# A transformer decoder in one program: biases added in PSUM and a new order in the first attention, and logits with standing weights

## The reference

```python
def _L0_attn_ref(x, ...):                      # 16 heads of 16
    q_in = linear(x, Wq_w, Wq_b).transpose(0, 2, 1)
    Q3 = conv1d(q_in, convq_w, convq_b, (1, 1))
    Q = linear(concat([q_in, Q3]), qproj_w, qproj_b)        # K likewise
    V = linear(x, Wv_w, Wv_b)
    tau = sigmoid(conv1d(gelu(conv1d(x_conv, tau1_w, tau1_b, groups=D)), tau2_w, tau2_b))
    # delta likewise
    scores = einsum('bhqd,bhkd->bhqk', Q, K) / sqrt(DK) * tau[..., None] + delta[:, :, None, :]
    out = einsum('bhqk,bhkd->bhqd', softmax(scores), V)
    return linear(out, out_w, out_b)
...
def _L0_ffn_ref(x, W_router, b_router, ...):
    logits = x_flat @ W_router.T + b_router                 # 4096 tokens, 8 experts, top 2
...
def _L1_ffn_ref(x, gate_query, log_temp, ...):
    gate_logits = einsum('bnd,ed->ben', x, gate_query)      # 16 experts
    affinity = _sinkhorn(gate_logits / exp(log_temp))
```

## Time and profile before

| | us |
|---|---|
| median of 3 runs | 2656.15 (2645.31 to 2673.6) |
| profiled execution | 2657.47 |
| its span | 2655.8 |
| granted TensorE clock, share of full speed, over the span | 0.912 |

### The profile page before, as it was taken

How to read it: one execution, slowest core, us unless ns; L and a number is a source line. 1 busy time by engine, 2 the same in 40 slices (tenths; PEclk the granted TensorE clock), 3 DMA queues, 4 the chain that set the end, 5 groups by cost and what they waited for, 6 DMA issues and landing times. The chain is left out here.

```text
span 2655.8 us, 46285 instructions
## 1 busy us (share of the span) xinstructions
PE 2191.8 (83%) x16966; PEld 1564.2 (59%) x16966; DVE 1637.7 (62%) x3322; ACT 1190.9 (45%) x1892; POOL 1057.1 (40%) x1203
## 2 busy tenths in 40 slices
PE   7588888887677729993899997995299999999996
PEld 6355555554455617872566666885167676767674
DVE  4578777785788665651777764555655555555552
ACT  1344445553211216651555553323264647474742
POOL 3976677660000012313555411210244545454533
PEclk9799999998887759996999997996599999999998
DMA  4000000000000113321001100003143434343422
GB/s 205 1 1 1 0 0 0 0 0 1 9 6 5 64 66 121 124 92 42 25 24 27 21 1 15 15 10 126 57 109 97 99 97 99 97 99 97 99 66 32
DMA packets 62560, 135.92 MB, mean 51 GB/s; under 512 B 10688, under 2 KB 46736, under 8 KB 55568
## 3 DMA queue, kind: packets, MB, share of 16 engines
q0 software_dynamic: 30976, 52.45, 9.7%
q1 hardware_dynamic: 31504, 82.41, 8.9%
HBM read 100.22 MB, written 34.60 MB: 51 GB/s over the span
## 5 line engine op out<-in xcount | busy, mean ns | idle before, releaser
L2957 ACT ACTIVATE f_h<-bank,f_b 128x512 f32<-128x512 f32 x256 | 175.9, 687 | 280.5 <-PE bank L176 273.3
L176 PE MATMUL ring<-f_w2hi,f_hidhi 128*128 128x256 f16 x1024 | 280.0, 273 | 6.0 <-DVE f_hidlo L2994 3.7
L2994 DVE TENSOR_TENSOR f_hidlo<-f_h,f_hidhi 128x512 f16<-128x512 f32 x256 | 177.3, 692 | 173.2 <-ACT f_hidhi L2958 172.0
L176 PE MATMUL ring<-f_w2hi,f_hidlo 128*128 128x256 f16 x1024 | 279.9, 273 | 0.0
L176 PE MATMUL ring<-f_w2lo,f_hidhi 128*128 128x256 f16 x1024 | 279.8, 273 | 0.0
L3048 POOL DMA_INDIRECT out<-f_y,f_to_row x128 | 211.8, 1655 | 47.7 <-issue 34.1
L176 PE MATMUL bank<-f_xthi,f_w1hi 128*128 128x512 f16 x512 | 195.2, 381 | 4.9 <-DVE f_w1lo L2977 4.9
L176 PE MATMUL bank<-f_xtlo,f_w1hi 128*128 128x512 f16 x512 | 195.1, 381 | 0.0
L176 PE MATMUL bank<-f_xthi,f_w1lo 128*128 128x512 f16 x512 | 195.1, 381 | 0.0
L1755 POOL COPY c_from_row<-c_token 128x5 uint32 (+1 forms) x8 | 1.5, 184 | 435.0 <-POOLq L1482 356.3
L2958 ACT ACTIVATE f_hidhi<-bank,f_b 128x512 f16<-128x512 f32 x256 | 173.9, 679 | 0.0
(11 more groups left out here) (519 smaller groups left out, 6001.7 us busy)
## 6 DMA issues: line engine op xcount, KB each, us to landing
f_raw<-in_e_w SPq DMA_DIRECT2D x32, 1024.0 KB
c_raw<-in_e_w SPq DMA_DIRECT2D x16, 1024.0 KB, 6.0
slots_out<-c_y POOLq DMA_DIRECT2D x8, 640.0 KB, 3.7
x<-in_x SPq DMA_DIRECT2D x1, 4096.0 KB, 23.9
tokens<-c_xn SPq DMA_DIRECT2D x16, 256.0 KB, 2.3
out<-x SPq DMA_DIRECT2D x1, 4096.0 KB, 13.7
tokens<-f_xn SPq DMA_DIRECT2D x16, 256.0 KB, 2.2
wb<-in_wb SPq DMA_DIRECT2D x1, 3096.0 KB, 31.8
```

The costliest lines, as they stand in the source:

```text
L176: mm = pe.matmul(out, left[a], right[b], start=first and n == 0, stop=last and n == 2)
L2957: act.activation(h32[n % 4][:, :], src, ACT.Gelu_apprx_tanh, bias=bias).then_inc(sig["h_full"], 1)
L2994: dve.tensor_tensor(hid_v[1][:, it, at], h32[n % 4][:, :], hid_v[0][:, it, at], ALU.subtract).then_inc(sig["h_lo"], 1)
```

## The change

In `attention_weights` DVE also splits the two rows of biases (v and output) into three bf16 parts that add up to them, and puts part k into partition k of `bias_parts`; POOL fills `ones`. In the attention a product of `ones` with `bias_parts`, accumulated into the same PSUM bank, adds the bias. The normalisation, v's copy and one of the four copies of weighed values go from DVE to ACT, and all three orders change. The logits of both stages come from one class, `EntryLogits`: the weights, padded to 32 columns, are loaded, and x moves in 256 columns, four entries side by side in four column tiles; the result, experts by tokens, is turned back. It has sixteen xn, written out without loops, and the stores are waited for one block later (`choose_experts`, `choose_tokens`). The store of x comes after those of xn.

```diff
@@ attention_weights, DVE @@
+                order.step(dve.tensor_copy(thirds[0][:, :], both))
+                order.wait()
+                order.step(dve.tensor_tensor(left[:, :], both, thirds[0][:, :], ALU.subtract))
+                order.wait()
+                order.step(dve.tensor_copy(thirds[1][:, :], left[:, :]))
+                order.wait()
+                dve.tensor_tensor(thirds[2][:, :], left[:, :], thirds[1][:, :], ALU.subtract)
+                order.step(dve.tensor_scalar(parts, thirds[0][:, :], here[:, 0:1], None, ALU.mult))
+                for k in (1, 2):
+                    order.wait()
+                    order.step(dve.scalar_tensor_tensor(out=parts, in0=thirds[k][:, :], scalar=here[:, k:k + 1],
+                                                        in1=parts, op0=ALU.mult, op1=ALU.add))
@@ first_attention, PE @@
+                def bias(out, n):
+                    return pe.matmul(out, mem.ones[:, :], mem.bias_parts[:, n * D:(n + 1) * D], start=False, stop=True)
...
                 def half(u, i, w, j, w_before, v):
                     rows(u, i, 0, w_before)
+                    if w_before:
+                        turn_weighed(other(u), w_before)
                     if v:
                         turn_x(u, v, w_before)
                     rows(u, i, 1, w_before)
-                    if w_before:
-                        turn_weighed(other(u), w_before)
                     rows(u, i, 2, w_before)
+                    if w:
+                        project_qk(w, j, 0)
                     if w_before:
                         turn_o(other(u), w_before, v)
-                    if w:
-                        project_qk(w, j, 0)
                     rows(u, i, 3, w_before)
                     if w:
                         project_qk(w, j, 1)
...
+                    rows(u, i, 6, w_before)
+                    if w:
+                        tau_delta(w, j, v)
+                    rows(u, i, 7, w_before)
+                    if w:
+                        project_qk(w, j, 4)
+                        sum_tau_delta(w, j)
+                        project_qk(w, j, 5)
+                    turn_again(u, i)
+                    if w:
+                        project_qk(w, j, 6)
+                        project_qk(w, j, 7)
+                    columns_of_scores(u, i, w, j, w_before, 0)
                     if w_before:
                         output(other(u), w_before)
+                    for c in (1, 2, 3):
                         columns_of_scores(u, i, w, j, w_before, c)
+                    weigh(u, i, 0)
+                    if w:
+                        turn_queries(w, j, 1)
+                    columns_of_scores(u, i, w, j, w_before, 4)
+                    if w:
+                        project_v(w, j)
+                    columns_of_scores(u, i, w, j, w_before, 5)
+                    weigh(u, i, 1)
+                    columns_of_scores(u, i, w, j, w_before, 6)
+                    if w:
+                        turn_queries(w, j, 0)
+                    columns_of_scores(u, i, w, j, w_before, 7)
+                    weigh(u, i, 2)
+                    if w:
+                        for t in (1, 0):
+                            turn_keys(w, j, t)
                     weigh(u, i, 3)
@@ first_attention, ACT: norm, copy_v and copy_weighed are new @@
                     if v:
+                        norm(u, v)
                         pad_x(u, v)
-                    if w:
-                        gelu(w, j)
                     if w_before:
                         copy_o(other(u), w_before)
                     if w:
+                        gelu(w, j)
...
+                    exponentials(u, i, 0)
+                    if w:
+                        high_queries(w, j)
+                    for c in range(1, 5):
                         exponentials(u, i, c)
                     if w:
-                        high_queries(w, j)
-                    for c in range(4, HP):
+                        copy_v(w, j)
+                    for c in range(5, HP):
                         exponentials(u, i, c)
                     if w:
                         copy_turned_keys(w, j)
+                    copy_weighed(u, i, 2)
@@ first_attention, DVE, the new lines of half (removed ones left out) @@
                     maximum(u, i, 0)
                     if w_before:
                         divide(other(u), w_before)
+                    for s in range(1, 8):
+                        maximum(u, i, s)
+                    stack_maxima(u, i)
+                    if w:
+                        take_td(w, j)
+                        take_q(w, j)
+                    copy_again(u, i)
+                    if w:
+                        scale_queries(w, j)
+                        take_k(w, j)
+                        stack_queries(w, j)
+                    if w_before:
+                        update(other(u), w_before)
+                    if w:
+                        stack_keys(w, j)
+                    take_weighed(u, i, 0)
+                    if w:
+                        copy_queries(w, j, 1)
                     if v:
                         low_x(u, v)
                     take_weighed(u, i, 1)
                     if w:
+                        copy_queries(w, j, 0)
                         copy_keys(w, j)
                     take_weighed(u, i, 3)
@@ EntryLogits @@
+            for h in range(KT):
+                for p in range(self.R):
+                    mm = pe.matmul(bank[4 + g % 2][32 * p:32 * p + 32, 0:S], self.w[:, h * 32:(h + 1) * 32],
+                                   tiles(self.xn_t[g % 2][p][:, :], KT)[:, h, :], start=h == 0, stop=h == KT - 1,
+                                   tile_position=(0, 32 * p), skip_group_check=True)
...
+        for g in range(G + 2):          # PE
+            if g < G:
+                turn(g)
+            if 1 <= g <= G:
+                multiply(g - 1)
+            if g >= 2:
+                turn_back(g - 2)
...
+        norm(0)                         # DVE
+        for g in range(1, G):
+            norm(g)
+            copy_by_expert(g - 1)
+            if g >= 2:
+                take(g - 2)
+        copy_by_expert(G - 1)
+        for g in (G - 2, G - 1):
+            take(g)
```

More of the change, by code:

```diff
@@ L263, in attention_weights @@
         cb = ctx.enter_context(nc.sbuf_tensor("fold_cb", [P, 2 * KT * P], F32))
+        thirds = [ctx.enter_context(nc.sbuf_tensor(f"fold_third{k}", [P, 2 * D], BF16)) for k in range(3)]
+        left = ctx.enter_context(nc.sbuf_tensor("fold_left", [P, 2 * D], F32))
         banks = mem.banks
@@ L782, in half @@
                         project_qk(w, j, 1)
-                    if w_before:
-                        output(other(u), w_before)
                     rows(u, i, 4, w_before)
@@ L1387, in router_logits @@
+def router_logits(nc, mem, dram, xn, logits, stored):
+    with ExitStack() as ctx:
+        work = EntryLogits(nc, mem, dram, "c", xn, ctx, tiles(mem.w("router"), KT), E0, stored)
+        by_entry = logits[:, :].rearrange("q (b t e) -> q b t e", t=NT, e=E0)
         with nc.Block() as block:
@@ L1405, in _ @@
             @block.scalar
             def _(act):
[L1407 to L1412 removed]
+                work.scalar(act)
             @block.sync
             def _(sp):
[L1416 to L1420 removed]
@@ L1432, in pair @@
-                def pair(i, now, last):
-                    if not last:
-                        norm(now)
-                    for p in range(R):
-                        dve.wait_ge(sig[f"logits_made{p}"], now)
-                        for t in range(NT):
-                            ins = dve.tensor_tensor(logits[:, bass.ds((i * R + p) * NE + t * E0, E0)],
-                                                    bank[R + p][:, t * E0:(t + 1) * E0], mem.row("router"), ALU.add)
-                        ins.then_inc(sig[f"logits_ready{p}"], 1)
@@ L1442, in _, with finish @@
-                norm(0)
-                in_pairs(dve, pair, B // R)
-def choose_experts(nc, mem, logits, token):
+                def finish(g, turned):
+                    for t in range(NT):
+                        ins = dve.tensor_tensor(by_entry[:, g * work.R:(g + 1) * work.R, t, :], turned[:, :, t, :],
+                                                mem.row("router").unsqueeze(1).to_broadcast([P, work.R, E0]), ALU.add)
+                    return ins
+                work.vector(dve, finish)
@@ L1451, in choose_experts @@
+def choose_experts(nc, mem, logits, token, stored):
     with ExitStack() as ctx:
```

345 lines of the change are left out of this document (163 added, 182 removed).

## The result

The changed kernel takes 2564.86 us (median of 4 runs, 2561.98 to 2567.87); the kernel before took 2664.88 in the same session (4 runs, 2645.31 to 2675.47). The ratio is 0.9619, its 95% interval 0.9579 to 0.9659. The forecast was 2581, range 2558 to 2618.

| stretch | before | after | less | forecast |
|---|---|---|---|---|
| to the first stack of maxima (weights, fold, front) | 112.95 | 112.20 | 0.8 | −0.5 |
| first to last stack of maxima | 529.46 | 461.72 | 67.7 | 55.5 |
| to the router's first norm | 260.18 | 261.99 | −1.8 | 0.7 |
| router, to the first reduction of choose_experts | 29.72 | 20.49 | 9.2 | 6 |
| to the gate's first norm | 872.03 | 870.27 | 1.8 | gate: 13.5 |

A forecast was written before the change was run, and what follows sets the result against it. The bound was PE waiting for DVE, DVE for POOL, POOL for x. Attention 55.5, last update 0.7, fold −0.5, router 6, gate 13.5 sum to 75.2 us off 2657.5: 2582.3, median-adjusted to 2581, range 2558 to 2618.

The forecast's parts named there:

- the bound is a ring: First attention: PE waits for DVE, DVE for POOL, POOL for x, which PE turns; PE stands 6.8 of 36.2 us a half.
- What leaves DVE: Attention: normalisation, output and v bias adds and one copy leave DVE, 5.7 of 28.5 us a half; ACT rises to 20.
- Bias products: Attention: four bf16 bias products of 256 columns added to PE, 0 to 0.95 us a half, taken as 0.45.
- Waits: Attention: PE's waits for xn (2.0), query stack (1.0) and second query copy (0.9) go; about 2 us a half stays.
- none over 0.6 us in its place: Sign in the attention: PE's wait for xn gone and no wait over 0.6 us replacing it.
- rival B: Chance 0.25: waits taken from PE come back elsewhere, POOL lengthening other DVE instructions; attention half 34.4, total 2612 us.
- PE's own work: Attention: PE's work taken as 29.4 + 0.45 us a half; up to 0.6 from a kept clock left to the range.
- Logit stages: Router and gate: standing weights and moving x save 9 or 2 us and 17 or 10; taken as 6 and 13.5.
- A: Rival, chance 0.52: the summed terms hold, 2581 us (2562 to 2602), attention half 31.5 to 33 us.
- C: Rival, chance 0.12: both logit stages stay at half clock, gaining 2 + 10 instead of 19.5 us; total 2589 us.
- D: Rival, chance 0.04: turning weighed values straight after rows 0 stalls PE and halves its clock; half 38.7, total 2675 us.
- E: Rival, chance 0.07: better than the sum, full clock throughout and an attention half of 30.5; 2560 us or less.

The follow-up runs named there:

- the square above: Table of attention halves: kernel before 36.2 us, with DVE relieved only 34.2, with the new order only 32.1, with both (the changed kernel) 30.8.
- the order alone: Changed kernel with normalisation, v's bias and the output's bias back on DVE, new order kept: 2576.39 us, ratio 0.9668.
- the relief of it: Kernel before, old order and old logits, with biases added in PSUM and normalisation on ACT: 2657.20 us, ratio 0.9974.
- POOL's pause: Changed kernel, with POOL waiting before two additions of convolution part 1 until DVE has stacked the maxima: 2544.38 us, ratio 0.9538.

## Why the prediction was right, point by point

**The bound.** That PE stood for waits in order, and that the order could cover them, was right and is shown by the square above: the order alone takes 2.8 of PE's 6.8 idle us a half, the granted clock is 1.00 with it, and xn made by DVE costs 0.05 us a half. Where I wrote "the bound is a ring", I gave DVE's load too much room: with the order old, the relief of it took 1.5 of the 6.8. And "busy without a gap" fits the router only: in the gate stage of before PE works 28.69 of 35.77 us.

**What leaves DVE.** I had 5.7 us a half leaving; 4.3 left: the two short stacking instructions took 2.0 more, and others, first of all the build of the query stack, took less. ACT's normalisation takes 0.60 each, not 0.42; ACT works 19.7 (20 forecast).

**Bias products.** 0.45 us a half for four; two of them are worth 0.21 at the end of the study. The number was right, by some luck: output() is four products in the code, which the trace records as eight, so the row gave 0.47 a product and not 0.24.

**Waits.** Idle 2.6 against 2.1 forecast. The exponentials are 0.9 and not 0.5, and the stacking wait of 1.0 was not in the sum. My test "none over 0.6 us in its place" therefore failed on two counts. It was B's mechanism: rival B was priced from what DVE had lost in all, as if POOL took the same from the path again; it took what one short instruction before `turn_again` is worth. The Trainium skill, page "SBUF — State Buffer", section "SBUF: two separate sides", says that DVE and GpSimd share a port pair, that a DVE instruction takes it when it reads two tiles in SBUF or runs in a two-port mode, and that whichever engine starts first holds it for its whole instruction while the other, if it needs the pair, is blocked. The timelines agree for DVE: 32 columns took 1.29 us when POOL's 1.27 us addition had started 0.07 us earlier, and 0.24 when it started 0.04 later. In that second case POOL's addition was not lengthened, it took 1.27 as ever; so that the short instruction held POOL up is not shown. DVE instructions that read two tiles do seem to: in the front of before, VectorE, then POOL, an instruction of POOL that takes 0.55 at its other places there took 1.48.

```profile
88.58 0.84 DVE L1006 SCALAR_TENSOR_TENSOR a_qs<-a_qf,a_td 128x256 f32<-128x256 f32 x2
```

```profile
88.81 1.48 POOL L925 TENSOR_SCALAR a_dw<-x_pad,cols 128x256 f32<-128x256 f32 x1
```

So my "alone" for L1027's 0.70 at 90.77 was a misreading: POOL was at work then, and it was POOL that waited.

**The mis-sized term of the attention** is PE's own work. The sum took 29.4 + 0.45 and left the clock's gain to the range; measured are 28.2. The trace of before had the price, in two of its halves (windows view, columns as in the earlier trace rows):

```profile
252.80:289.00 36.20, 28.39 (x314) 18.92 (x312) 29.75 (x49) 17.95 (x20) 24.54 (x34) 1.00 0.00 0
289.00:325.00 36.00, 30.46 (x304) 19.43 (x303) 27.47 (x43) 17.62 (x19) 24.53 (x34) 0.91 0.00 0
```

PE's work at clock 1.00 is 28.4, not 29.4. Counted from stack to stack, PE works 3.0 us less in the first of these halves than in the second (28.05 against 31.07), and yet the half is only 0.8 shorter (35.86 against 36.61), since PE stands longer: in before the waits swallow most of what the clock gives, and a half whose waits are covered keeps it. With 28.4 + 0.45 + 2.1 the half would have been 30.95; measured 30.82. That is 1.05 × 11 = 11.6 of the 12.2 us by which the attention beat the forecast. I had carried up to 0.6 for it, in the range alone, though its condition, that PE no longer stands 2 us at a time, stood in my own text.

**Fold.** 0.5 forecast; the last bias_k starts 0.23 later. **First and last intervals**: 122.0 forecast, 122.7 measured.

**Logit stages.** At full clock I had 9 and 17; measured 9.2 and 16.6 (14.9 and the 1.8 before it). I took the middle for a doubt that did not come true: DVE's thread does leave PE gaps of 1.0 to 1.2 us a group, and the clock stays at 1.00. For the switches of the array's tiling I carried nothing, and PE's answer, forecast at 1.64 us a group (0.44 + 0.2 + 1.0), took 1.78: over eight groups 1.1 us more, not 3. Against it, copy and take, forecast at 1.02 a group, cost 0.54.

**What the sum did not see** is that its base was a favourable execution: 2657.47 us, where the median with one more run is 2664.88. So the gain is 100.0 by medians and 94.4 by the two profiles. The old router, as one cause, was seen at 29.7 us in the kernel before and at 42.1 in two others with the same stage; whether the kernel or the execution decides is not shown, as each has one profile. The new form of the router, unedited, took 20.36 to 20.49 in six of seven profiles and 19.82 in the other (POOL's pause). What makes before's 32 us of spread in one session stays open too: its attention took 529.5 us in one profile and 525.0 in another with the same code.

**Rivals.** A held in its total (2562 to 2602) and its mechanism, but its half of 31.5 to 33 was missed: the 30.8 measured lie nearer to E's. B's mechanism was there, at less than half its price. C did not occur. D's place, the turning of the weighed values, costs 0.3 us a half. E's condition, full clock throughout, was met, with 30.8 a half instead of 30.5.

## What to carry to other kernels

Cover a wait by putting work of the waiting engine ahead of it before taking load off the engine that is waited for; here, from first to last stack, the first was worth 46 to 50 us and the second 15 to 20. When a change removes the stalls that halve the clock, price the waiting engine's work from a window at full clock. And when one engine's short instruction is on the path, look at what the neighbour that shares its port starts at that moment: a wait that costs the neighbour 0.87 us a half was worth 13 us of the whole.

## What the runs showed of the hardware that was not expected

- The same code of the router stage ran for 42.08 us at granted clock 0.50 in two kernels, and for 29.72 at 0.73 in another, with PE shown busy 40.70 and 28.34 us. In all four profiles of a router with small products behind loads of 128 columns (8 columns moving) PE is busy 88 to 97% of the stage, and the granted clock is 0.50 twice, 0.69 and 0.73. In the changed kernel, with tiled products of 256 columns and gaps of 1.0 to 1.2 us a group, it is 1.00 from 842 to 856 us.
- A DVE instruction on 32 columns takes 0.24 or 1.29 us, depending on whether POOL's addition of 512 columns started 0.04 us after or 0.07 us before it.
- Issues of stores behind a 4 MB store take 22.86 us for sixteen instead of 15.77 (without the waits for xn 14.3 instead of 5.5), so a store that nobody waits for can still delay a barrier through the engine that issues it.
